# Attribute rows of a graph kernel's sort: loads in blocks of 112, 15 and 1 partitions, record numbers joined by a transfer, pauses of GpSimd in the scatter

## The reference

```python
# layer 0, twice:  msg = x[src] * weight;  agg = segment_sum(msg, dst) + x;  leaky(x @ Ws + (agg / cnt) @ Wn)
# layer 1:         h_agg = mean over row of (x[col] @ W_msg + b);  relu([x @ W_lin, h_agg] @ W_upd)
# layer 2:         aggregated = segment_sum(edge_attr, dst);  silu(layernorm([x, aggregated] @ W1)) @ W2
# layer 3, twice:  h_ref = x[src] - 2 * dot * rel[type];  layernorm(x + (segment_sum(h_ref, dst) / deg) @ W)
edge_index = jnp.stack([src, dst])
x = _layernorm(x + _L0(x, edge_index, edge_weight, ...), axis=-1)
x = _layernorm(x + _L1(x, edge_index, ...), axis=-1)
x = _layernorm(x + _L2(x, edge_attr_128, edge_index, ...), axis=-1)
x = _layernorm(x + _L3(edge_index, edge_type_1001, x, ...), axis=-1)
```

## Time and profile before

| | |
|---|---|
| median of 3 runs | 4971.06 us (4969.9 to 4978.57) |
| profiled execution | 4971.85 us |
| its span | 4970.0 us |
| TensorE matmul, busy | 3726.0 us (75%) |
| VectorE, busy | 3443.7 us (69%) |
| GpSimd, busy | 2967.1 us (60%) |
| ScalarE, busy | 2168.6 us (44%) |
| DMA | 887.00 MB, mean 178 GB/s |

### The profile page before, as it was taken

The page is one execution under the profiler, slowest core; times in us unless marked ns, Lnnn a source line. Parts: engine busy times, 40 slices in busy tenths (PEclk is TensorE's granted clock), DMA queues, the critical chain, the costliest instruction groups (busy, mean ns, idle before and its releaser), DMA issues.

```text
span 4970.0 us, 92754 instructions
## 1 busy us (share of the span) xinstructions
PE 3726.0 (75%) x18848; PEld 2300.1 (46%) x18956; DVE 3443.7 (69%) x13252; ACT 2168.6 (44%) x4510; POOL 2967.1 (60%) x3448
## 2 busy tenths in 40 slices
PE   4650019999977899877899798899678775688776
PEld 1220004447843355533566688888523443234443
DVE  8860027545675487764576688888888788987888
ACT  0000002673314588844455344444326555155666
POOL 2432335436767599877233366666667577675877
PEclk6775559999989999999999999999889998899999
DMA  1111134668844688644788555555447776477776
GB/s 53 46 46 40 41 53 144 213 231 271 279 131 142 210 270 262 226 133 155 240 269 269 176 172 170 167 166 166 130 140 223 235 228 207 120 219 237 236 229 193
DMA packets 551185, 887.00 MB, mean 178 GB/s; under 512 B 106502, under 2 KB 161429, under 8 KB 550765
## 3 DMA queue, kind: packets, MB, share of 16 engines
q1 hardware_dynamic: 361242, 609.56, 38.9%
q10 hardware_dynamic: 135427, 168.59, 9.8%
q0 software_dynamic: 54096, 104.47, 7.8%
HBM read 545.11 MB, written 337.20 MB: 178 GB/s over the span
## 4 chain that ended last, share of the span: by engine, by line
PE 34%; DVE 18%; ACTq 13%; issue 10%; POOL 8%; DVEq 7%; DMA 5%; SPq 3%; ACT 1%; POOLq 0%; another core or an unknown queue 0%
ACTq L1233 13%; PE ps L1493 12%; DVEq L68 6%; POOL got L680 5%; DVE stat L1073 4%; PE ps L1616 3%; PE ps L1615 3%; DVE hit L1021 3%; PE ps L1521 2%; PE ps L1625 2%; DVE hid L1174 2%; PE ps L1553 2%; PE ps L1552 2%; DVE mv L1079 2%; POOL x2T L696 2%
## 5 line engine op out<-in xcount | busy, mean ns | idle before, releaser
L716 POOL TENSOR_TENSOR rstd<-vare,neg_half 128x4 f32<-128x4 f32 x686 | 699.4, 1020 | 620.4 <-DVE vare L1086 617.6
L1289 ACT ACTIVATE xout<-res,shift,rstd 128x128 f32<-128x128 f32 x1176 | 482.9, 486 | 425.7 <-POOL shift L719 409.9
L1493 PE MATMUL ps<-hit,got 128*128 128x512 bf16 x1148 | 457.5, 399 | 239.4 <-DVE hit L1021 118.9
L1114 DVE TENSOR_TENSOR nT<-sums,ps 128x512 f32<-128x512 f32 x490 | 335.8, 685 | 350.5 <-PE ps L1531 286.5
L1493 PE MATMUL ps<-hit,rest 128*128 128x512 bf16 x1148 | 457.4, 398 | 98.5 <-DVE hit L1021 97.4
L1264 ACT ACTIVATE evac<-ps 128x512 f32<-128x512 f32 x392 | 234.1, 597 | 675.5 <-PE ps L1493 659.4
L680 POOL DMA_INDIRECT got<-nodes_l,sorted_by_dst x392 | 398.4, 1016 | 159.7 <-issue 105.5
L1493 PE MATMUL ps<-hit,tail 128*128 128x512 bf16 x1148 | 456.0, 397 | 1.4 <-issue 0.2
L1493 PEld LDWEIGHTS ps<-hit,got 128*128 x1172 | 118.5, 101 | 583.3 <-issue 486.1
L1249 ACT ACTIVATE ps<-zeros 128x512 f32<-128x512 f32 x588 | 344.2, 598 | 29.5 <-SPq L414 7.6
L680 POOL DMA_INDIRECT got_pair<-in_x,sorted_by_dst x196 | 198.4, 1012 | 200.8 <-PE ps L1493 127.6
(11 more groups left out here) (265 smaller groups left out, 10237.2 us busy)
## 6 DMA issues: line engine op xcount, KB each, us to landing
nodes_l<-xout SPq DMA_DIRECT2D x196, 256.0 KB
xin<-nodes_l SPq DMA_DIRECT2D x196, 256.0 KB, 2.7
sums<-sums_l SPq DMA_DIRECT2D x196, 256.0 KB
sums_l0a<-evac_pair ACTq DMA_DIRECT2D x98, 256.0 KB
sums_l<-evac_pair ACTq DMA_DIRECT2D x98, 256.0 KB
sums<-sums_l0a SPq DMA_DIRECT2D x98, 256.0 KB
sums_l0b<-evac ACTq DMA_DIRECT2D x98, 256.0 KB
sums<-sums_l0b SPq DMA_DIRECT2D x98, 256.0 KB
```

The costliest lines, as they stand in the source:

```text
L716: pool.tensor_tensor(rstd[:, n, at, :], vare[:, n, at, :], neg_half[:, :], ALU.pow)\
L1114: dve.tensor_tensor(nT[:, slot % 4, :], sums[:, slot, :], ps[:, bank + slot % 2, :], ALU.mult).then_inc(s["nT"].sem, 1)
L1289: last = act.activation(dest[:, slot % ring, k, :], rows[:, slot % rows.shape[1], k, :], ACT.Identity, bias=shift[:, n, at, k:k + 1], scal ...
L1493: last = pe.matmul(into, part.rearrange("p a d -> p (a d)"), w.hit[:, i % w.hits, :], start=False, stop=False, skip_group_check=True)
```

## The change

Three things, all in the sort by `dst`:

- `attr_parts` cuts the 127 partitions into a transfer of 112 and one of 15; the single partition stays as it is.
- The record's eight words get into the row by a transfer within SBUF, issued on ScalarE's queue behind the batch's attribute loads and counted with them on `s_row`. Before the first load ScalarE's queue waits for `s_record`. The copy on GpSimd and its wait are gone.
- At every fourth batch (b = 3, 7, ..., 47) GpSimd fills a small tile `pause` and drains, before it waits for the batch's rows.

```diff
+        pause = front("pause", [P, 100])
         row = front("row", [P, ROW_RING, K, FIELDS + D], I32)
@@ attr_parts
-            parts = [(held[0:FULL_PARTS, :, :], v[0:full, :].rearrange("(p k) d -> p k d", k=TILES)[:, k:k + K, :])]
+            whole = v[0:full, :].rearrange("(p k) d -> p k d", k=TILES)
+            parts = [(held[lo:hi, :, :], whole[lo:hi, k:k + K, :]) for lo, hi in ((0, P - 16), (P - 16, FULL_PARTS))]
@@ rows_in
-            return 16 * sum(1 + (i * K + K <= REST) for i in range(b % ROW_RING, b + 1, ROW_RING))
+            return 16 * sum(3 + (i * K + K <= REST) for i in range(b % ROW_RING, b + 1, ROW_RING))
@@ as_placed (GpSimd)
-                if b == 0:
-                    held(s_record, 1)
                 if b % 7 == 0:
                     held(s_place, b // 7 + 1)
-                pool.wait_ge(s_row[b % ROW_RING], rows_in(b))
-                pool.tensor_copy(row[:, b % ROW_RING, :, 0:FIELDS], record[:, b * K:b * K + K, :]).then_inc(s_joined, 1)
-                held(s_joined, b + 1)
+                if b % 4 == 3:
+                    pool.memset(pause[:, :], 0.0)
+                    pool.drain()
+                held(s_row[b % ROW_RING], rows_in(b))
                 return lambda k: row[:, b % ROW_RING, k % K, :]
@@ ScalarE's queue
+                if b == 0:
+                    act.wait_ge(s_record, 1)
                 for part, ap in attr_parts(b):
                     act.dma_start(part, ap).then_inc(s_row[b % ROW_RING], 16)
+                act.dma_start(row[:, b % ROW_RING, :, 0:FIELDS], record[:, b * K:b * K + K, :]).then_inc(s_row[b % ROW_RING], 16)
```

More of the change, by code:

```diff
@@ L328, in program @@
         s_row = [sem(f"s_row{b}") for b in range(ROW_RING)]
-        s_joined = sem("s_joined")
         s_scattered = sem("s_scattered")
```

## The result

The changed kernel takes 4640.32 us in the median of four runs (4638.74 to 4642.03), beside 4970.48 us for the kernel before: ratio 0.9334, 95% interval 0.9317 to 0.935. The profiled execution took 4638.74 us, 333.1 us less than that of before.

A forecast was written before the change was run, and what follows sets the result against it. Attribute loads on one DMA engine bound the first stage; then GpSimd's path, 58.8 + 250.9 + 99.5 + 12 = 421.2 us, plus reload, starts L940 at 439.7 us, 267.8 us earlier: 4703 us, range 4655 to 4745 us.

The forecast's parts named there:

- first scatter: GpSimd's first scatter was to start at 58.8 us, with place ready at about 58.3 us and the copy gone.
- 196 scatters at the bare pace: GpSimd's scatters in the first stage: 1.28 us each, 250.9 us in all.
- last scatter's end: Last scatter of the sort by `dst`: start, scatters, pauses and blocking were to sum to 421.2 us.
- landing and reload: After the last scatter: 1.8 us to the reload's issue and 16.7 us for the reload, as before.
- What bounds the kernel: First stage: a single file of attribute loads of about 13 us, 49 batches, on one always busy DMA engine.
- Blocks on many engines: Loads cut 112, 15 and 1: all transfers 35.3 us of engine time per batch, 2.2 us over 16 engines, below 5.1 us.
- Issues and later start: ScalarE's queue: 1.4 us of issues a batch, first load at 40.3 us in place of 21.7 us; cost nothing.
- The pause: GpSimd's memset and drain every fourth batch: drain 7.58 us, 8.3 us a pause, 99.5 us for twelve.
- VectorE in the way: Scatters slowed by VectorE's `member` work: 10 us lost, plus 2 us for other two-input work, 12 us.
- Rival A: Drain within the scatter cheap: 4616 us at 0.31 us, 4664 us at 4.30 us; chance 0.13 cheap, 0.11 between.
- Rival B: Attribute loads stay on one DMA engine, which becomes slower: 5015 us, or 5368 us with record numbers there too; chance 0.04.
- Rival C: Scatters slower under DMA traffic, 1.378 us each: 19 us more, 4722 us; counted inside the forecast's 0.68.

## Why the prediction was wrong

By its own steps, in its order:

| step | forecast | measured in the changed kernel |
|---|---|---|
| first scatter | 58.8 us | 60.1 us |
| 196 scatters at the bare pace | 250.9 us | 196 x (0.962 + 0.305) = 248.3 us |
| twelve pauses | 99.5 us | 31.6 us |
| scatters blocked by VectorE | 12 us | 15.2 us, what is left |
| last scatter's end | 421.2 us | 355.2 us |
| landing and reload | 18.5 us | 18.4 us |
| L940 | 439.7 us | 373.6 us |

The pauses: twelve gaps, 32.6 us in all, and 2.7 us of memsets, less 12 x 0.305 us. The forecast put L940 66.1 us too late; this one term was 67.9 us too large, and the others together 1.8 us too small.

- **What bounds the kernel**: right. The load of 127 partitions kept one DMA engine busy; 113 brought its pace back, 126 and 112 did not. The Trainium skill's rule that was weighed there (page "DMA: Bandwidth & Descriptors", section "Why a DMA increments its semaphore by 16 and not by 1") gives 1 engine for 113 and 14 for 126. The runs agree with it: 11.8 us from load to load for the one, loads that never hold GpSimd up for the other; that it was 14, no run here shows.
- **Blocks on many engines**: right. From 100 to 200 us q10 used 19.5% of 16 engines, 312 us of engine time for 16.7 batches, thus some 19 us a batch (forecast: 14.4 + 7.7), and the scatter 13.7 us (forecast: 13.2): 2.0 us a batch over 16 engines, well under 5.1 us.

```profile
q10 hardware_dynamic: 17528, 4.63, 19.5%
q0 software_dynamic: 2048, 4.46, 13.7%
```

- **Issues and later start**: right, they cost nothing (0.5 and 0.64 us each rather than 0.34, three or four a batch, still ahead of the scatter).
- **The pause**: this step failed. I took the drain's price from rows of stages with 196 indirect DMAs, 7.58 us, and applied it to 16. I had named the ground to doubt it, that fewer DMAs may leave less to do, and gave it 0.13 and 0.11 for in between. The measured price is 1.8 us from the memset's end. For 16 DMAs the count alone asks for 1.36 us; the drain also waits for the landing of the last one, and ends 0.70 us after it. The row at 2109.6 us, with no DMA before it and 0.31 us, fits the low end of the line: it ended at 2109.91 us, 0.12 us after GpSimd's last instruction.
- **VectorE in the way**: right in kind, a little low: three scatters at 4.76 us and some shorter hits. VectorE's own work ended at 344.4 us, 9.8 us later than before, and was no bound, as said; without the pauses it became one.
- **Rival A** (a cheap drain) was the one that came, in a middling form; it gave 4664 us for 4.30 us a drain and 4616 us for 0.31 us, and the measured 4640 us lies between. My range reached down to the first of them only. **Rival B** did not occur; its cheap form was tried by the uncut load with the transfer, and was no slower than before. The Trainium skill's rule against cutting a transfer (page "DMA: Bandwidth & Descriptors", section "Rules for kernel authors") has a premise that fails here, as that load didn't use all engines: cut, it was worth 323 us. **Rival C** did not occur: the median scatter stayed at 0.962 us.
- **A step that was missing**: the tile. Its place alone is worth 17 to 20 us in the kernel before. It didn't move this result, since the loads it speeds up are no longer on the path.

## What to carry to other kernels

When every piece of a queue's chain is one long issue, multiply the queue's share of 16 engines by 16. If that gives one engine, suspect that the partition count can't be dealt out; here a block of 112 or 126 with the rest apart mended that. A price measured at a stage's end may carry the whole stage in it: before it is multiplied, look for what it grows with, and widen the range to the other end until that is known. Once the large wait is gone, what was hidden in it (a copy and its wait of 1 us a batch, a drain) is on the path and worth taking out: without pauses the kernel takes 4607 us, as fast as any here, and then VectorE's own work sets the stage's end.

## What the runs showed of the hardware that I had not expected

A GpSimd drain after indirect DMAs that have all landed costs 0.06 us and 0.0815 us for each of them since the last drain (4 to 108 measured); a memset between doesn't reset that, another drain does. Where they have not all landed and are few (4 to 16), it ends 0.22 to 0.70 us after the landing of the last one. After 196 of them it is 7.57 us, less than the 8.87 us after 108. Moving the destination of a load by 448 bytes changed its time from 12.71 to 12.28 us. And in two of the five sets TensorE stood while loads ran on many engines. In the worse one it stood for some 11 us at a time with no engine of the core to wait for; that cost the first stage more than 200 us, and more than half of the gain.
